# Second attention of a two-layer gated transformer block: the output bias as two one-row products of TensorE

## What is computed

```python
x = x + tanh(g_xattn[0]) * L0_xattn(layernorm(x), ctx)          # 16 heads of 64
x = x + tanh(g_ffn[0])   * L0_ffn(layernorm(x))                 # quantised
x = x + tanh(g_xattn[1]) * L1_xattn(layernorm(x), ctx, mask)    # 16 heads of 16
x = x + tanh(g_ffn[1])   * L1_ffn(layernorm(x))                 # shared expert + top 2 of 8

def L1_xattn(d, e, mask):        # in words: q, k, v with biases, 16 heads
    score = q @ k.T / sqrt(16) * mask; score[score == 0] = -1e9
    context = softmax(score) @ v
    return context @ wo_w + wo_b                                # wo_b: 256 numbers
```

## Time and profile before

| | before |
|---|---|
| median of 3 runs (lowest to highest) | 1660.81 us (1658.57 to 1665.26) |
| the profiled execution | 1660.71 us, of which 1658.9 us from its first to its last instruction |
| busy: PE, PEld, DVE, ACT, POOL | 1402.6, 998.6, 1237.2, 1107.8, 210.1 us |
| mean granted clock of PE | 0.936 of full speed |
| second attention | from 859 to 1328 us of the span |
| its loop of slots | from 883 to 1327 us |

### The profile page before, as it was taken

The page is one execution under the profiler, slowest core; times in us unless marked ns, Lnnn a source line. Parts: engine busy times, 40 slices in busy tenths (PEclk is TensorE's granted clock), DMA queues, the critical chain, the costliest instruction groups (busy, mean ns, idle before and its releaser), DMA issues. The chain is left out here.

```text
span 1658.9 us, 40477 instructions
## 1 busy us (share of the span) xinstructions
PE 1402.6 (85%) x15436; PEld 998.6 (60%) x15436; DVE 1237.2 (75%) x3092; ACT 1107.8 (67%) x2445; POOL 210.1 (13%) x185
## 2 busy tenths in 40 slices
PE   1699999999999996294186989898988879999996
PEld 1466766677666665252174666666666557788884
DVE  6478888887888886949767999889888877344443
ACT  5467777777777774257516888888888744366663
POOL 4501000000010000400003000000000010034443
PEclk9999999999999999598597999999999979999998
DMA  4122323322323221000010212121010072212221
GB/s 146 56 62 93 108 90 97 96 84 83 109 83 115 74 71 42 29 1 26 0 56 11 82 48 80 52 76 34 18 34 12 5 252 65 63 32 49 46 47 23
DMA packets 64911, 105.69 MB, mean 64 GB/s; under 512 B 7434, under 2 KB 38899, under 8 KB 63571
## 3 DMA queue, kind: packets, MB, share of 16 engines
q1 hardware_dynamic: 58002, 94.83, 18.2%
q0 software_dynamic: 6720, 8.27, 3.1%
HBM read 68.88 MB, written 35.11 MB: 63 GB/s over the span
## 5 line engine op out<-in xcount | busy, mean ns | idle before, releaser
L1326 ACT ACTIVATE a_p<-a_s,a_nb 112x375 f32<-112x375 f32 x256 | 140.9, 598 | 26.6 <-DVE a_nb L1440 26.3
L294 PE MATMUL a_ps_o<-a_vh,a_pt 125*128 125x64 f16 (+1 forms) x1536 | 152.7, 183 | 2.7 <-ACT a_pt L1339 0.8
L1247 PE MATMUL a_ps_t<-ident,a_p 112*128 112x112 f32 x768 | 117.0, 282 | 42.8 <-ACT a_p L1326 41.7
L296 PE MATMUL a_ps_o<-a_vh,a_pt 125*128 125x64 f16 (+1 forms) x1536 | 151.1, 182 | 0.0
L295 PE MATMUL a_ps_o<-a_vl,a_pt 125*128 125x64 f16 (+1 forms) x1536 | 151.0, 182 | 0.0
L583 ACT ACTIVATE a_p<-a_ps_s,a_nb 112x375 f32<-112x375 f32 x256 | 143.8, 572 | 3.5 <-DVE a_scaled L674 3.5
L591 ACT ACTIVATE a_pt<-a_ps_t 125x336 f16<-125x336 f32 x256 | 101.8, 448 | 66.1 <-PE a_ps_t L522 65.7
L294 PEld LDWEIGHTS a_ps_o<-a_vh,a_pt 125*128 125x128 f16 x1536 | 133.4, 97 | 14.9 <-ACT a_pt L1339 6.7
L1247 PEld LDWEIGHTS a_ps_t<-ident,a_p 112*128 112x128 f32 x768 | 78.8, 144 | 97.5 <-issue 82.6
L295 PEld LDWEIGHTS a_ps_o<-a_vl,a_pt 125*128 125x128 f16 x1536 | 130.7, 98 | 11.0
L1440 DVE CUSTOM_DVE_ANT_0 a_s<-a_s,a_fill 112x375 f32<-112x375 f32 x256 | 129.9, 545 | 5.5
(11 more groups left out here) (428 smaller groups left out, 4544.9 us busy)
## 6 DMA issues: line engine op xcount, KB each, us to landing
a_piece<-in_w SPq DMA_DIRECT2D x72, 256.0 KB, 3.1
split_weights<-a_pair SPq DMA_DIRECT2D x72, 256.0 KB, 3.4
w<-split_weights SPq DMA_DIRECT2D x8, 1024.0 KB, 6.1
a_ctx<-in_ctxT SPq DMA_DIRECT2D x16, 375.0 KB, 3.7
ctx<-a_cx SPq DMA_DIRECT2D x16, 375.0 KB, 4.4
a_cx<-ctx SPq DMA_DIRECT2D x16, 375.0 KB, 5.8
w1h<-split_weights SPq DMA_DIRECT2D x2, 1792.0 KB, 14.0
w1l<-split_weights SPq DMA_DIRECT2D x2, 1792.0 KB, 16.4
```

The source lines that it names most:

```text
L294: nc.tensor.matmul(out, wh, mh, start=(i == 0), stop=False)
L296: last = nc.tensor.matmul(out, wl, mh, start=False, stop=(i == n - 1))
L1247: mm = nc.tensor.matmul(ps_t[:, 2 * (g % 2) + i, t * S:(t + 1) * S], p32[:, g % 2, i, t * KV:t * KV + 128], ident32[0:S, 0:S], start=(t == ...
L1326: nc.scalar.activation(p32[:, g % 2, i, 0:NC], s2[:, g % 2, i, :], ACT.Exp, bias=nb[:, g % 2, i:i + 1], scale=-1.0).then_inc(exp_done, 1)
```

## The change

`bo` is now one row. From it ACT makes `bo_hi`, the float16 part of 32 times the bias, and DVE `bo_lo`, the rest. POOL fills a row `unit` of 112 numbers with 32 after its other constants. Job W begins with two matmuls whose weights are `unit` (1 row, 112 columns) and which stream `bo_hi` and `bo_lo` (1 row, 256 columns), so that the PSUM bank holds 1024 times (product + bias) at the end; the following six matmuls are those of `products`, in the same order. `bo_g`, the 16 additions by POOL with their waits for `bo_scaled` and `normed`, and DVE's 16 waits for `bo_added` go. ACT's `bo_hi` stands ahead of its part of the first Q and waits for the DMA of the bias; DVE's `bo_lo` stands where `bo_g` was made, and waits for ACT. PE waits for `unit` once, ahead of the first W.

```diff
-        bo, bo_g = sb("a1_bo", [S, D]), sb("a1_bo_g", [S, D])
+        bo, bo_hi, bo_lo = sb("a1_bo", [1, D]), sb("a1_bo_hi", [1, D], F16), sb("a1_bo_lo", [1, D], F16)
+        unit = sb("a1_unit", [1, S], F16)
...
-            sp.dma_start(bo[:], A["L1_xattn_wo_b"].partition_broadcast(S)).then_inc(small_in, 16)
+            sp.dma_start(bo[:], A["L1_xattn_wo_b"].partition_broadcast(1)).then_inc(small_in, 16)
...
-                    last = products(nc, ps_j[0:S, 0:D], [
-                        (oth[:, k, :], otl[:, k, :], wo[:, 0, k, :], wo[:, 1, k, :]) for k in range(KD)])
+                    if b == 0:
+                        pe.wait_ge(unit_made, 1)
+                    nc.tensor.matmul(ps_j[0:S, 0:D], unit[:], bo_hi[:], start=True, stop=False)
+                    nc.tensor.matmul(ps_j[0:S, 0:D], unit[:], bo_lo[:], start=False, stop=False)
+                    for k in range(KD):
+                        nc.tensor.matmul(ps_j[0:S, 0:D], oth[:, k, :], wo[:, 0, k, :], start=False, stop=False)
+                        nc.tensor.matmul(ps_j[0:S, 0:D], oth[:, k, :], wo[:, 1, k, :], start=False, stop=False)
+                        last = nc.tensor.matmul(ps_j[0:S, 0:D], otl[:, k, :], wo[:, 0, k, :], start=False,
+                                                stop=(k == KD - 1))
...
+            act.wait_ge(small_in, 16)
+            nc.scalar.activation(bo_hi[:], bo[:], ACT.Copy, scale=WS).then_inc(bo_high, 1)
             act.wait_ge(zeroed, Q_CONSTS)
...
-            pool.wait_ge(bo_scaled, 1)
-            for b in range(B):
-                pool.wait_ge(normed, b + 1)
-                nc.gpsimd.tensor_tensor(x_res[:, b, :], x_res[:, b, :], bo_g[:], ALU.add).then_inc(bo_added, 1)
+            nc.gpsimd.memset(unit[:], WS).then_inc(unit_made, 1)
...
                     dve.wait_ge(job_done, i + 1)
-                    dve.wait_ge(bo_added, b + 1)
...
-            dve.wait_ge(small_in, 16)
-            nc.vector.tensor_scalar(bo_g[:], bo[:], tanh_g[0:S, 1:2], None, ALU.mult).then_inc(bo_scaled, 1)
+            dve.wait_ge(bo_high, 1)
+            link(nc.vector.scalar_tensor_tensor(out=bo_lo[:], in0=bo[:], scalar=WS, in1=bo_hi[:], op0=ALU.mult,
+                                                op1=ALU.subtract))
```

More of the change, by code:

```diff
@@ L1107, in attention1_phase @@
                  "pt_hi", "hi_taken", "pt_lo", "pv_done", "job_done", "q_masked", "job_hi", "job_lo", "o_ready",
-                 "chain", "bias_ready", "bo_scaled", "bo_added", "bias_landed", "var_ready", "std_ready", "normed")
+                 "chain", "bias_ready", "bo_high", "unit_made", "bias_landed", "var_ready", "std_ready", "normed")
         (small_in, zeroed, own_made, scored, masked, max_ready, exp_done, p_transposed, pt_hi, hi_taken, pt_lo,
-         pv_done, job_done, q_masked, job_hi, job_lo, o_ready, chain, bias_ready, bo_scaled,
-         bo_added, bias_landed, var_ready, std_ready, normed) = (sem(f"a1_{n}") for n in names)
+         pv_done, job_done, q_masked, job_hi, job_lo, o_ready, chain, bias_ready, bo_high, unit_made, bias_landed, var_ready, std_ready, normed) = (sem(f"a1_{n}") for n in names)
         ctx_in = [sem(f"a1_ctx_in{i}") for i in range(2)]
```

## The result

| | before | after |
|---|---|---|
| median of 4 runs (lowest to highest) | 1660.49 us (1658.57 to 1665.26) | 1682.39 us (1676.60 to 1685.84) |
| ratio to before, 95% interval | | 1.0115 (1.0094 to 1.0135) |
| profiled execution's span | 1658.9 us | 1681.5 us |
| first to last operation of DVE on W | 925.9 to 1327.2: 401.3 us | 926.6 to 1349.7: 423.1 us |

The change makes the kernel slower by 22 us between the medians, 1.3% (1.15% or 19 us by the ratio in the table), where +1.0 us was forecast. In the profiled executions the spans differ by 22.5 us, and 21.8 of them lie between the first and the last W, inside the loop of slots.

What follows compares the result with a forecast made beforehand. PE, DVE and ACT form a ring, none alone the bound; PE sets the pace behind 1.2 GHz Ws. Of 2.2 + 0.4 = 2.6 us, 2.2 come back; 0.42 at the end plus 0.6 give +1.0: 1661.8 us, range 1656 to 1668.

Steps and rivals of the forecast that it cites:

- the cost of W: Two added matmuls per W: 0.22 us in each of ten 1.2 GHz batches of the loop, 2.2 us; 0 at 2.4 GHz.
- The raster: In the loop, clock falls that meet a W come 27.3 us or a multiple apart, within 0.1 us.
- What is given back: In the loop, longer slow batches drift faster, so one or two more fast batches return the 2.2 us.
- Depth buys next to nothing: In W, a one-row matmul costs like W's own: 0.212 us at 1.2 GHz, 0.11 at 2.4.
- The slack of a 2.4 GHz W: In five 2.4 GHz batches, PE's added 0.22 us lies in 1.0 us of slack: 0, bound 1.1 us in all.
- The last W: At the loop's end, at 1.2 GHz with nothing behind to hide the two matmuls: +0.42 us.
- rival 1: In the loop, nothing is given back: +2.6 to +5.7 us, 1663.4 to 1666.5 us; chance 0.23.
- The range: Whole kernel: 1656 to 1668 us, to hold the forecast and 1666.5 us with the earlier executions' spread.
- POOL's side and the start: Removing POOL's 16 additions: 0, bound -0.6 us; making `bo_hi` and `bo_lo` at the start, inside waits: 0.
- Rival 2: The clock falls ahead of every W, so fast batches are lost: +11.2 us, 1672.0 us; chance 0.07.
- Rival 3: The clock no longer falls at W, as PE has more to do there: 1649.1 us; chance 0.03.

Runs made afterwards that it cites:

- e4: Kernel before plus six full-depth matmuls whose result nobody reads, filling PE's idle gap ahead of the transposes in W's slot: 1660.6 us, ratio 0.9999.
- e2: Kernel before without POOL's 16 additions and DVE's waits for them, the output bias left out: 1660.0 us, ratio 0.9993.
- e1: Changed kernel with the two bias products 128 rows deep instead of one, same columns and order: 1664.3 us, ratio 1.0023 to the kernel before.
- e6: Changed kernel plus 18 unread full-depth matmuls filling PE's gaps in the slots of W and V0: 1659.0 us, ratio 0.9981 to the kernel before.
- e5: Kernel before plus unread full-depth matmuls filling two PE gaps, six in W's slot and twelve in V0's: 1654.3 us, ratio 0.9953.
- e12: Kernel before with the gaps in the slots of W and V0 filled by 7 and 14 unread full-depth matmuls: 1653.3 us, ratio 0.9943.
- e13: Changed kernel with bias products 128 rows deep, unit weights 32 in one row and 0 in 127: 1663.5 us, ratio 1.0019 to the kernel before.
- e14: Kernel before plus a single unread one-row matmul of 16 columns ahead of W's six products, POOL's additions kept: 1672.0 us, ratio 1.0059.

## Why the prediction was wrong

**The step that failed** stands in the cost of W: "what is pushed past that moment is done at 2.4 GHz, if, as I take it, the moment stays". It doesn't. I had read from the trace when the clock falls and had argued that the fall comes ahead of W and so is left alone by the change. There are indeed no more falls: between 900 and 1300 us seven in after, ten in before. Of the five in after that meet a W, three come ahead of it and two just behind the start of its first one-row product. I then took the end of the stretch as given, and never asked what PE has to do for it to end. In after it ended 13.7 us after the fall, not 3.4, in all three stretches with the whole of W in them. The trace of before could have warned: its stretches at 1.2 GHz at the start and at the end of this phase lasted 20.5 and 23.9 us (from 872.4 and from 1319.6), so no fixed length could be assumed.

**The raster** of 27.3 us held in the traces of before and e4, and not in that of after: its falls between 900 and 1300 us come 58.0, 30.7, 85.3, 10.2, 20.5 and 71.7 us apart. In e2, which only lacks POOL's additions, they come 20.5 and 61.4 us apart beside the 27.3. So "What is given back" rested on an order that this one execution had. One reading beside it was the wrong way round: by rows 7 the batch of 26.44 us begins behind a W at 2.4 GHz and ends behind one at 1.2 GHz. The sum doesn't hang on it.

**"Depth buys next to nothing"** was right for the duration and was carried over to the clock, where it isn't. The rule of the Trainium skill that I weighed (page "TensorE: Matmul & The Clock Gate", section "LDWEIGHTS (loading the stationary operand)") speaks of durations alone. On those it agrees with after as far as the load itself goes: 121 ns at the least for one row, against 126 to 130 for 128 rows. What neither tells is the pause beside a shallow product, 0.18 us in a W at 2.4 GHz (eight steps of after take 1.05 us, of e1 0.87) and 0.09 us ahead of it (0.19 against 0.10).

**The slack of a 2.4 GHz W** was taken as 0 with a bound of 0.22 us. By e6 and e5 it is the bound: 26.67 against 26.45 us.

**The last W** was priced at 0.42 us at 1.2 GHz; its two products took 0.60.

**What is given back.** In e1, where only length was added, the profiled loop took 401.6 us from the first W to the last, against 401.3, and the falls inside it became nine from ten. That is what I forecast for the change. Yet e1 is 3.8 us slower in the median, inside rival 1's range; in that one execution 1.9 us of it lie ahead of the first W and 1.3 behind the last. Whether executions differ there by the change or by chance stays open.

**The range**, 1656 to 1668 us, left 1.5 us above rival 1's 1666.5, though the spread it names is 4.5 us. The 1682.4 us lie outside of either.

**POOL's side and the start** were right: e2 gives 0 for the additions, and `bo_hi` and `bo_lo` are hidden.

**The rivals.** None had this mechanism. Rival 2 had the sign, by more falls; their number went down. Rival 3, that the clock would no longer fall at W, was wrong for the change. Its price of 12 us was right: the profiled execution of e5, without a fall in the loop, is 12.9 us shorter than that of before. The medians of e5 and e12 are 6 to 8 us lower. My reasons for its small chance named the gap ahead of W, and that gap was the thing to fill.

## What to carry to other kernels

A product of one row (a bias, a mask, a rank-one term on TensorE) is not priced by its columns alone. Ask in what stretch of the granted clock it stands: at a steady 2.4 GHz it cost its time and the pauses around it (some 0.2 us a batch here); in a stretch at 1.2 GHz it held the clock down for up to four times as long. If such a product is wanted, give it the full 128 rows, with weights repeated or zero; that took 18 of the 22 us away here. Where a trace shows falls behind idle gaps of PE, try to fill *all* of the gaps with deep matmuls that nobody reads: here one filled gap only moved the fall, two gave 0.5%.

## What the runs showed of the hardware

- Where W began at most 1.3 us behind the fall and had two one-row products, the stretch at 1.2 GHz lasted 13.7 us in 23 of 23 cases; with these products 128 rows deep 3.4 us in 14 of 14; with 64 rows 3.4 us in three and 13.7 in four. The medians by depth: 1682 (1 row), 1688 (32), 1674 (64), 1664 us (128).
- Weights that are zero in 127 of 128 rows do as well as full ones (e13, 1663.5 us against 1664.3): the length of the stretches goes by the rows of the instruction, not by the values of its weights.
- One matmul of one row and 16 columns in each W, 0.21 us long, cost 11 us over the kernel (e14).
- Beside products of 1, 32 or 64 rows PE steps by 0.15 to 0.20 us at 2.4 GHz and 256 columns, where it otherwise steps by 0.11. The pauses are the same for the three depths.
- The longest pause of PE between 900 and 1300 us of before is 1.45 us, and the clock fell ten times there.
- Open: why one one-row product is worse than two (1692 against 1682 us), why 32 rows are no better than one (the scores, 32 rows deep, stand in every slot of every kernel), why two stretches of the same kind differ with 64 rows, and how pause and streaming share the harm.
